# A Householder step that takes its norm and its diagonal element out of the matrix product, on one Trainium2 core

## The reference

```python
deg = jnp.sum(A, axis=0) + jnp.sum(A, axis=1) - jnp.diagonal(A)
d_inv_sqrt = jnp.where(deg > 0, jax.lax.rsqrt(deg), 0.0)
L = jnp.diag(deg) - A
L_norm = d_inv_sqrt[:, None] * L * d_inv_sqrt[None, :]
_, U = jnp.linalg.eigh(L_norm)
agg = jnp.einsum('mn,bnd->bmd', U.T, features)
h = jax.nn.relu(agg @ W1 + b1)
out = h @ W2 + b2
return jnp.einsum('nm,bmd->bnd', U, out)
```

## Time and profile before

| | |
|---|---|
| median of 3 runs | 6160.08 us (6158.68 to 6161.56) |
| the profiled execution, its own time | 6150.05 us |
| its span in the profile | 6147.9 us |
| first and last L969 (w of steps 0 and 509) | 895.1 and 3609.1 us into the span |
| PE, DVE busy over the span | 54%, 70% |
| ACT, POOL busy over the span | 15%, 13% |

### The profile page before, as it was taken

How to read it: one execution, slowest core, us unless ns; L and a number is a source line. 1 busy time by engine, 2 the same in 40 slices (tenths; PEclk the granted TensorE clock), 3 DMA queues, 4 the chain that set the end, 5 groups by cost and what they waited for, 6 DMA issues and landing times.

```text
span 6147.9 us, 78861 instructions
## 1 busy us (share of the span) xinstructions
PE 3290.3 (54%) x19000; PEld 2342.0 (38%) x19000; DVE 4304.7 (70%) x27212; ACT 932.4 (15%) x4314; POOL 790.6 (13%) x3424
## 2 busy tenths in 40 slices
PE   7877738888888888777777730000002212230476
PEld 4333226565566666666666630000002212120243
DVE  1222286666677777888888889999968888889534
ACT  2432201111122222222222210000000000000000
POOL 0000001111111111111100014444430000000000
PEclk9988855555555555555555555555555555565578
DMA  2000000000000000000000000000000000000000
GB/s 55 0 0 0 0 0 1 1 1 1 1 1 1 1 1 1 1 1 1 1 1 1 1 1 1 1 1 1 1 1 0 0 0 0 0 0 0 0 0 27
DMA packets 20805, 17.38 MB, mean 3 GB/s; under 512 B 6544, under 2 KB 16784, under 8 KB 20368
## 3 DMA queue, kind: packets, MB, share of 16 engines
q1 hardware_dynamic: 20368, 12.65, 0.8%
HBM read 8.41 MB, written 4.20 MB: 2 GB/s over the span
## 4 chain that ended last, share of the span: by engine, by line
DVE 53%; PE 37%; issue 6%; ACT 2%; SPq 1%; POOL 0%; DMA 0%; DVEq 0%; ACTq 0%; POOLq 0%
PE bank L487 9%; PE bank L436 5%; PE bank L499 5%; PE bank L491 3%; DVE qp L1193 2%; PE bank L470 2%; PE bank L438 2%; DVE ycol L934 2%; DVE dif L1546 2%; PE bank L482 2%; DVE ts L966 1%; DVE qp L1183 1%; DVE tau_row L950 1%; DVE jcol L958 1%; DVE gated L948 1%
## 5 line engine op out<-in xcount | busy, mean ns | idle before, releaser
L487 PE MATMUL bank<-lapw,hid 128*32 128x160 f32 (+3 forms) x10200 | 660.3, 421 | 61.2 <-DVE lapw L907 17.8
L524 PE MATMUL bank<-diag,blk 128*128 128x32 f32 (+1 forms) x96 | 23.3, 416 | 1041.4 <-DVE diag L1310 1030.0
L487 PEld LDWEIGHTS bank<-lapw,hid 128*32 128x32 f32 x10200 | 395.1, 163 | 190.7 <-DVE lapw L969 83.0
L499 PE MATMUL bank<-xp,ones 128*128 128x1 f32 x1020 | 298.9, 362 | 277.9 <-DVE xp L958 277.9
L524 PEld LDWEIGHTS bank<-diag,blk 128*128 128x128 f32 x96 | 21.4, 327 | 1043.5 <-DVE diag L1310 1031.9
L219 POOL TENSOR_TENSOR sq<-hid,ltm 128x4 f32<-128x4 f32 (+3 forms) x510 | 101.0, 198 | 2324.3 <-DVE hid L961 2265.7
L497 PE MATMUL bank<-xp,ones 128*128 128x1 f32 x1020 | 299.0, 362 | 185.4 <-DVE xp L940 185.4
L436 PE MATMUL bank<-hid,onehot 128*128 x504 | 328.2, 769 | 120.0 <-DVE ga L736 67.2
L499 PEld LDWEIGHTS bank<-xp,ones 128*128 128x128 f32 x1020 | 255.3, 311 | 321.6 <-DVE xp L958 321.6
L497 PEld LDWEIGHTS bank<-xp,ones 128*128 128x128 f32 x1020 | 255.3, 311 | 229.1 <-DVE xp L940 229.1
L470 PE MATMUL bank<-xn,ones 128*128 128x2 f32 x1020 | 299.3, 363 | 18.5 <-DVE xn L887 17.6
(11 more groups left out here) (729 smaller groups left out, 8493.1 us busy)
## 6 DMA issues: line engine op xcount, KB each, us to landing
out_x<-xs SPq DMA_DIRECT2D x16, 256.0 KB, 3.3
lapw<-in_adj SPq DMA_DIRECT2D x1, 1024.0 KB, 5.9
bias_rows<-in_L_gnn_bg SPq DMA_DIRECT2D x8, 64.0 KB, 5.6
hid<-lz SPq DMA_DIRECT2D x32, 1.0 KB, 1.7
bias_rows<-in_L_gnn_b SPq DMA_DIRECT2D x4, 64.0 KB, 5.7
wg<-in_L_gnn_Wg SPq DMA_DIRECT2D x2, 64.0 KB, 11.0
wg<-in_L_gnn_W SPq DMA_DIRECT2D x2, 64.0 KB, 3.6
xs<-in_x SPq DMA_DIRECT2D x1, 0.5 KB, 19.7
```

The source lines that it names most:

```text
L487: m = pe.matmul(bank[1][32 * q:32 * q + 32, 0:(T + 1) * 32].rearrange("p (u i) -> p u i", i=32), acols[:, t, k:k + 1].to_broadcast([P, 32] ...
L499: pe.matmul(bank[2][:, 4 * NB:4 * NB + 1], ones[:, 0:P], xp[:, 1:2], start=True, stop=True).then_inc(vp_ps, 1)
```

## The change

PE's product gets two more columns to work on. Before it starts, GpSimd writes the unit vector of row k+1 into the panel's free w place, and the masked column `am` (a without its first element) into the v place, so that the same product delivers a's diagonal element `alpha` and the sum of squares of the rest. DVE copies both out (`al`), and from them ScalarE forms the root and GpSimd the scalars `coef` (sign, sum of squares, its product with the sign, and a value with the check for a zero column folded in). The vector v is never formed: the panel holds `am`, and what v adds to it is a scalar `p` in the weights. DVE takes the product of a and y, and the elements of a1 and y in row k+1, as three columns `xd`, and one product with ones sums all three. The products with ones for the norm, the check and the second sum are gone (L470, L495, L499), and so are `norms`, GpSimd's squares and DVE's v. The next column is now formed before w by one operation from `am`. PE's product now waits for `w_ready`, `a_ready` and GpSimd's `am_ready`. After the loop, scalars that were columns before are put right in rows, and the shift is added to the stored columns.

The core of the diff; lines taken away from the loops of GpSimd, ScalarE and VectorE are those of the listing above and are left out, and so is the code after the loop.

```diff
@@ GpSimd @@
             for k in range(STEPS):
...
+                t0, j = (k + 1) // P, k % NB
+                T = NT - t0
+                if k == 0:
+                    pool.wait_ge(a_ready, 1)
+                else:
+                    pool.wait_ge(y_done, k)
+                if j == 0 and k:
+                    pool.wait_ge(panx_ps, k // NB)
+                pool.tensor_copy(pan[:, t0:, :, j, 0], onehot[:, t0:, k + 1].unsqueeze(2).to_broadcast([P, T, 4])).then_inc(am_ready, 1)
                 pool.wait_ge(a_ready, k + 1)
+                pool.tensor_tensor(pan[:, t0:, :, j, 1], acols[:, t0:, k].unsqueeze(2).to_broadcast([P, T, 4]),
+                                   ltm[:, t0:, k + 1].unsqueeze(2).to_broadcast([P, T, 4]), ALU.mult).then_inc(am_ready, 1)
+                pool.wait_ge(al_ready, k + 1)
+                pool.tensor_scalar(coef[:, 0:1], al[:, 0:1], 0.0, 0.5, ALU.is_ge, ALU.subtract).then_inc(coef_ready, 1)
+                pool.tensor_scalar(coef[:, 1:2], al[:, 0:1], al[:, 0:1], al[:, 1:2], ALU.mult, ALU.add).then_inc(coef_link, 1)
+                pool.wait_ge(coef_link, linked + 1)
+                pool.wait_ge(coef_ready, 3 * k + 1)
+                pool.tensor_tensor(coef[:, 2:3], coef[:, 1:2], coef[:, 0:1], ALU.mult).then_inc(coef_ready, 1)
+                pool.tensor_scalar(coef[:, 3:4], al[:, 1:2], 1e-24, 1e37, ALU.is_le, ALU.mult).then_inc(coef_link, 1)
+                linked += 2
+                pool.wait_ge(coef_link, linked)
+                pool.tensor_tensor(coef[:, 4:5], coef[:, 3:4], coef[:, 1:2], ALU.add).then_inc(coef_ready, 1)
@@ ScalarE @@
                     act.wait_ge(updated, k // NB)
+                if k == 0:
+                    act.wait_ge(a_ready, 1)
                 act.activation(tz[:, t0:, 0], lap[:, t0:, k + 1], ACT.Copy).then_inc(edge_ready, 1)
...
+                act.wait_ge(am_ready, 2 * k + 2)
+                act.activation(swap[:, t0:, j, 0], pan[:, t0:, 0, j, 1], ACT.Copy).then_inc(v2_ready, 1)
+                act.wait_ge(al_ready, k + 1)
+                act.activation(root[:, 0:1], al[:, 0:1], ACT.Sqrt, scale=al[:, 0:1], bias=al[:, 1:2]).then_inc(norm_root, 1)
+                act.wait_ge(norm_root, 2 * k + 1)
+                act.wait_ge(coef_ready, 3 * k + 1)
+                act.activation(root[:, 1:2], coef[:, 0:1], ACT.Copy, scale=root[:, 0:1]).then_inc(norm_root, 1)
+                act.wait_ge(p_ready, 2 * k + 2)
+                act.activation(w0[:, t0:], pcol[:, t0:], ACT.Copy, scale=th[:, 0:1]).then_inc(w0_ready, 1)
+                act.activation(p_row[:, k:k + 1], wts[:, 0:1], ACT.Copy)
+                act.activation(tau_row[:, k:k + 1], th[:, 0:1], ACT.Copy)
+                act.wait_ge(w_ready, k + 1)
+                act.activation(swap[:, t0:, j, 1], pan[:, t0:, 0, j, 0], ACT.Copy).then_inc(w2_ready, 1)
+                act.activation(ends_row[:, k, :], bank[3][:, 0:3:2], ACT.Copy).then_inc(vy_saved, 1)
             act.activation(tz[:, NT - 1:, 0], lap[:, NT - 1:, N - 1], ACT.Copy).then_inc(edge_ready, 1)
@@ TensorE @@
-                pe.wait_ge(norm_in, 2 * (k + 1))
-                pe.matmul(bank[0][:, 0:2], ones[:, 0:P], xn[:, 0:2], start=True, stop=True).then_inc(norm_ps, 1)
                 if k:
                     pe.wait_ge(w_ready, k)
-                    pe.wait_ge(v2_ready, k)
...
                     pe.wait_ge(updated, k // NB)
+                pe.wait_ge(a_ready, k + 1)
+                pe.wait_ge(am_ready, 2 * k + 2)
                 for t in range(t0, NT):
                     strips = lapw[:, t, c0:].rearrange("p (u q i) -> p u q i", q=4, i=32)
                     for q in range(4):
...
-                pe.wait_ge(tail_in, k + 1)
-                pe.matmul(bank[4][:, 0:1], ones[:, 0:P], xn[:, 2:3], start=True, stop=True).then_inc(tail_ps, 1)
-                pe.wait_ge(x_ready, k + 1)
-                pe.matmul(bank[3][:, 0:1], ones[:, 0:P], xp[:, 0:1], start=True, stop=True).then_inc(vy_ps, 1)
-                pe.wait_ge(x2_ready, k + 1)
-                pe.matmul(bank[2][:, 4 * NB:4 * NB + 1], ones[:, 0:P], xp[:, 1:2], start=True, stop=True).then_inc(vp_ps, 1)
+                pe.wait_ge(x_ready, 2 * k + 2)
+                pe.matmul(bank[3][:, 0:3], ones[:, 0:P], xd[:], start=True, stop=True).then_inc(vy_ps, 1)
@@ VectorE, before the loop @@
-            bcol_ = pole_gap
-            V.tensor_copy(bcol_[:, :, 0], lap[:, :, 0])
+            V.tensor_tensor(c4[:, 8:9], lap[:, 0, 0:1], ident[:, 0:1], ALU.mult)
             V.tensor_tensor(acols[:, :, 0], lap[:, :, 0], ltm[:, :, 0], ALU.mult).then_inc(a_ready, 1)
@@ VectorE, the loop @@
+                T, c0, e = NT - t0, t0 * P, (k + 1) % P
+                a_, here = acols[:, t0:, k], T * 32 + 2 * j
...
                 dve.wait_ge(y_done, k + 1)
+                V.tensor_scalar(al[:], bank[1][:, here:here + 2], 1e-36, None, ALU.add).then_inc(al_ready, 1)
                 a = put(V.tensor_tensor(yz[:, t0:, 0:32], bank[1][:, 0:T * 32].rearrange("p (t i) -> p t i", i=32),
                                         pick[:].unsqueeze(1).to_broadcast([P, T, 32]), ALU.mult))
                 if j:
                     dve.wait_ge(w2_ready, k)
...
                     a = put(V.tensor_tensor(yz[:, t0:, 32:32 + 2 * j], panel_cols(j, t0), panel_rows(bank[1][:, T * 32:T * 32 + 32], j, T), ALU.mult))
+                after(a)
+                y = put(V.tensor_reduce(ya[:, t0:, 1], yz[:, t0:, 0:32 + 2 * j], AX.X, ALU.add))
+                dve.wait_ge(edge_ready, k + 1)
+                if j:
                     rowz += 1
                     dve.wait_ge(rowz_ps, rowz)
...
+                    after(put(V.tensor_tensor(tz[:, t0:, 1:1 + 2 * j], panel_cols(j, t0), panel_rows(bank[2], j, T), ALU.mult)))
+                a1done = put(V.tensor_reduce(ya[:, t0:, 0], tz[:, t0:, 0:1 + 2 * j], AX.X, ALU.add))
+                after(y)
+                V.tensor_tensor_reduce(jcol[:, 0, t0:], a_, ya[:, t0:, 1], 1.0, 0.0, ALU.mult, ALU.add, xd[:, 2:3]).then_inc(x_ready, 1)
+                dve.wait_ge(norm_root, 2 * k + 1)
+                r = put(V.reciprocal(ts[:, 0:1], root[:, 0:1]))
                 after(a1done)
+                V.tensor_tensor(xd[:, 0:2], ya[:, t0, :], ident[:, e:e + 1].to_broadcast([P, 2]), ALU.mult).then_inc(x_ready, 1)
+                dve.wait_ge(norm_root, 2 * k + 2)
+                dve.wait_ge(coef_ready, 3 * k + 2)
+                after(r)
+                p = put(V.tensor_scalar(wts[:, 0:1], ts[:, 0:1], coef[:, 2:3], root[:, 1:2], ALU.mult, ALU.add))
+                dve.wait_ge(coef_ready, 3 * k + 3)
+                c = put(V.reciprocal(cn_row[:, k:k + 1], coef[:, 4:5]))
+                after(p)
+                q = put(V.tensor_scalar(ts[:, 1:2], al[:, 0:1], wts[:, 0:1], coef[:, 4:5], ALU.mult, ALU.add))
+                m = put(V.tensor_tensor(yam[:, t0:, :], ya[:, t0:, :], ltm[:, t0:, k + 1].unsqueeze(2).to_broadcast([P, T, 2]), ALU.mult))
+                after(c)
+                g = put(V.tensor_tensor(wts[:, 2:5:2], wts[:, 0:1].to_broadcast([P, 2]), cn_row[:, k:k + 1].to_broadcast([P, 2]), ALU.mult))
+                after(q)
+                V.reciprocal(th[:, 0:1], ts[:, 1:2]).then_inc(p_ready, 1)
+                after(m)
                 if k:
                     dve.wait_ge(w0_ready, k)
...
+                V.scalar_tensor_tensor(pcol[:, t0:], yam[:, t0:, 0], wts[:, 0:1], yam[:, t0:, 1], ALU.mult, ALU.add).then_inc(p_ready, 1)
+                dve.wait_ge(p_ready, 2 * k + 1)
+                h = put(V.tensor_scalar(th[:, 1:2], th[:, 0:1], th[:, 0:1], wts[:, 0:1], ALU.mult, ALU.mult))
+                dve.wait_ge(p_ready, 2 * k + 2)
                 after(g)
...
+                b = put(V.scalar_tensor_tensor(nbcol[:, t0:], pcol[:, t0:], wts[:, 4:5], yam[:, t0:, 0], ALU.mult, ALU.subtract))
                 dve.wait_ge(vy_ps, k + 1)
...
+                V.tensor_tensor_reduce(jcol[:, 1, 0:2], bank[3][:, 1:3], wts[:, 3:5], 1.0, 0.0, ALU.mult, ALU.add, zy[:, 0:1])
+                z = put(V.tensor_tensor_reduce(jcol[:, 2, 0:3], bank[3][:, 0:3], wts[:, 0:3], 0.5, 0.0, ALU.mult, ALU.add, zy[:, 1:2]))
+                after(max(z, h, b))
+                x = put(V.tensor_tensor(xk[:], zy[:], th[:], ALU.mult))
+                after(x)
+                am = pan[:, t0:, 0, j, 1]
+                V.scalar_tensor_tensor(acols[:, t0:, k + 1], am, xk[:, 0:1], nbcol[:, t0:], ALU.mult, ALU.subtract).then_inc(a_ready, 1)
                 dve.wait_ge(w0_ready, k + 1)
...
+                V.scalar_tensor_tensor(pan[:, t0:, :, j, 0], am.unsqueeze(2).to_broadcast([P, T, 4]), xk[:, 1:2], w0[:, t0:].unsqueeze(2).to_broadcast([P, T, 4]),
                                        ALU.mult, ALU.subtract).then_inc(w_ready, 1)
```

138 lines of the change are left out of this document (33 added, 105 removed).

## The result

The changed kernel takes 6272.45 us (median of 4 runs, 6247.99 to 6273.30) against 6159.38 us for the kernel before on the same chip (4 runs, 6154.14 to 6161.56). The ratio of the runs is 1.0175, with a 95% interval of 1.0150 to 1.0201, so the change is slower. By the medians it is +113 us, where the forecast was +50. The profiled execution was the fastest of the four, 6247.99 us with a span of 6246.2 us. Against the profiled execution of before that is +98 us, and it is these 98 us that the two traces can explain.

A forecast was written before the change was run, and what follows sets the result against it. No engine is full; a chain of waits in each step bounds the kernel. Stage changes of 15, 17, 22 and -8 us plus 3.5 gave +50: 6200 us against the profiled execution, 6210 against the median; range 6125 to 6310.

The forecast's parts named there:

- each sign of being right: DVE waits on L237 before L927 at T = 1 and 2, those steps level over j, L226 releasing PE's product.
- (4): GpSimd's scalars, from the start of `al` until DVE can use the last: 1.64 us, bounds 1.36 to 1.85.
- (5): DVE's own route from `al` to L927: 1.84 us at T = 4, j = 13, deciding there over GpSimd's 1.64.
- (3): Scalars moved behind the product: from L927 the column runs 1.45 to 1.67 us, PE starts at 2.02.
- The cut of a step: PE's product, from its start to DVE's first operation on it: 2.43, 1.58, 0.94, 0.51 us for T = 4 to 1.
- (1): Removing the v chain ahead of L924: worth nothing at T = 4 and 3, 0.18 us at T = 2, 0.61 at T = 1.
- (2): Step's end, PE also waiting for GpSimd's copy of `am`: 0.35 us from column's end to product, 0.15 lost a step.
- The base: Ordinary step lengths of the kernel before, as panel means: 6.08, 5.13, 4.43 and 4.23 us for T = 4 to 1.
- (6): Panel updates costed like ordinary steps; row operations and others behind the loop add 3.5 us; start of the loop nothing.
- GpSimd's scalars are dear: Rival: small TENSOR_SCALARs on GpSimd cost 0.36 us or more, scalars at 1.85 or later, +150 us, 6310; chance 0.20.
- rival C: GpSimd's scalars cheap at 0.195 us each, DVE's list decides nearly everywhere: -16 us, 6144, up to -100, 6060; chance 0.20.

The follow-up runs named there:

- the control: The changed kernel run again with nothing altered, against the kernel before on the same chip: 6258.3 us against 6157.6, ratio 1.0165.

## Why the prediction was right or wrong

The sign, the mechanism and the place of the waits were right; the size was half of what came. The first profile agrees with each sign of being right that the forecast named: L927 follows L237's end by 0.03 us with T = 1 and 2 at every j, steps there are level over j, and PE's product is released by L226. What failed are sizes: (4), (5) and (3), each by some hundredths of a us in a step, over 510 steps. By the forecast's parts:

- **The cut of a step was right.** From PE's start to `al` it is 2.42, 1.56, 0.93 and 0.50 us (medians by stage in the control) where the forecast had 2.43, 1.58, 0.94 and 0.51.
- **(1) What v's removal is worth** is borne out by that: `al` follows the product's end by 0.06 in every stage. But the shorter product of T = 1, where most was to be won (0.61), is spent whole by what is new.
- **(2) and (3)** The part from L927 to PE is 2.02 with T = 1, exactly the sum. It comes of two errors that cancel: from the column's end to PE it is 0.43, not 0.35 (3412.63 to 3413.06, since PE starts 0.14 behind GpSimd's end, not the 0.06 that was taken from DVE), and DVE's part ahead of it is shorter by as much. With T = 4 it is 2.11 (in the step behind the one shown) and 0.09 were missing, as in the medians of the control (2.11, 2.05, 2.03 and 2.02 by stage).
- **(4) GpSimd's scalars, the term that decides, was mis-sized.** 1.71 to 1.72 us from `al` to L927 with T = 3 to 1, not 1.64. The durations were good (231, 341 and 235 ns, for 0.25, 0.37 and 0.25 us). What failed is the gap: the forecast let L234, which depends on nothing ahead of it, start 0.03 before the end of L233, from the one row pair L239 to L240. It starts 0.08 behind it (3410.42 to 3410.50, and 0.084 in the median of all 510). That pair was of another kind, a TENSOR_TENSOR behind a TENSOR_SCALAR. The 0.11 lost there, less what the durations gave back, are the 0.07.
- **(5) DVE's own route was also mis-sized**: 1.91 with T = 4, j = 13, not 1.84. Up to L917 it is 1.35, forecast 1.33; from there to L925 it is 0.37, forecast 0.31, with L925 0.22 behind the start of L921. L925 has several semaphores to wait for. That this is the cause wasn't tried.
- **The base was taken with its stalls, the sum without.** The panel means of the kernel before, 4.43 and 4.23 with T = 2 and 1, hold stalls of some steps; the medians of its ordinary steps are 4.41 and 4.20. The new step, built from gaps, had no stalls. The real one has: in the step with T = 4 shown, L940 starts 0.25 later than in the next one (1311.98 behind L938 at 1311.61, against 1318.44 behind 1318.32). Starts on DVE that come at least 0.15 later than usual add up to 12 us over the ordinary steps before and to 13 in the control. So stalls are part of what the sum lacked, but not of what the change costs.
- **(6) and behind the loop**: steps with j = 0 went up by 0.2 to 0.4 in T = 4 to 2, somewhat more than the ordinary ones, and by 0.13 in T = 1. Of the 3.5 us behind the loop 0.8 show in the first profile and 3.2 in the control's; two executions of one kernel differ by as much.

Added up, an ordinary step came 0.11 (T = 4, 6.31 against 6.20), 0.09, 0.08 and 0.08 over the forecast; over 127 or 128 steps each that is 46 us, less the 2.7 that didn't show behind the loop; the remaining 5 of the missing 48 are the panel steps and rounding. By the means of the first profile the way from `al` to L927, parts (4) and (5), has 31 us of the 46, and the way from L927 to PE, part (3) with the stalls, 25, most of it with T = 4 and 3; the product gives 8 back. By the medians the forecast lacks not 48 but 63 us. The other 15 lie between the profiled executions and the medians of the two kernels, and no trace shows where.

So the rival "GpSimd's scalars are dear" was wrong in its price (1.85) and rival C, "DVE's list decides", wrong in its sign. What can be seen only behind the experiments: GpSimd's wait, undone in part by moving one operation, was worth 62 us, and DVE's tail, which the forecast named as a sum of parts (2.02) but never as the thing to shorten, 104.
